# Attention block in fp16 pairs: row maxima of two heads at once on 64 rows each, and (1 + tanh) z on VectorE

## What is computed

```python
xn = jax.nn.silu(group_norm(x, gn_scale, gn_offset))        # 32 groups
qkv = jnp.einsum('bxyc,cd->bxyd', xn, w_qkv)
q, k, v = (to_heads(t) for t in jnp.split(qkv, 3, axis=-1))
sim = jnp.einsum('bhdi,bhdj->bhij', q * HEAD_CH ** (-0.5), k)
attn = jax.nn.softmax(sim, axis=-1)
out = jnp.einsum('bhij,bhdj->bhid', attn, v)
...
return jnp.einsum('bxyd,dc->bxyc', out, w_out) + b_out + x
```

## Time and profile before

| | us |
|---|---|
| median of 3 runs | 3589.93 |
| lowest and highest | 3588.99 and 3590.62 |
| the profiled execution | 3591.17 |
| its span | 3589.4 |
| PE busy | 3527.4 |
| VectorE busy | 2936.4 |
| ScalarE busy | 2738.4 |
| GpSimd busy | 2415.1 |

### The profile page before, as it was taken

One profiled execution on the slowest core, in us unless ns is written; L12 is line 12 of the kernel. 1 busy time (PEld: TensorE's weight loads), 2 busy tenths in 40 slices (PEclk: granted clock), 3 DMA queues, 4 the chain that ended last, 5 costly groups with the idle time before them and its releaser, 6 DMA issues.

```text
span 3589.4 us, 91303 instructions
## 1 busy us (share of the span) xinstructions
PE 3527.4 (98%) x31822; PEld 2074.5 (58%) x31822; DVE 2936.4 (82%) x3763; ACT 2738.4 (76%) x3076; POOL 2415.1 (67%) x2238
## 2 busy tenths in 40 slices
PE   6999999999999999999999999999999999999998
PEld 3555555565555556556565555555556555555555
DVE  7788878888788887888878888788888888878778
ACT  3787877878778787777877778787787877878776
POOL 1594866849578494775948659486684957849555
PEclk8999999999999999999999999999999999999999
DMA  3313323233232322223233232331323223232232
GB/s 97 71 36 97 68 42 94 54 83 65 50 86 53 83 65 64 72 59 93 48 73 80 45 97 42 97 68 42 95 53 83 65 52 85 53 83 65 43 92 47
DMA packets 178014, 245.82 MB, mean 68 GB/s; under 512 B 53536, under 2 KB 86304, under 8 KB 177568
## 3 DMA queue, kind: packets, MB, share of 16 engines
q1 hardware_dynamic: 177568, 239.94, 28.1%
HBM read 88.35 MB, written 33.82 MB: 34 GB/s over the span
## 4 chain that ended last, share of the span: by engine, by line
PE 89%; DVE 3%; POOL 3%; issue 3%; ACT 2%; DMA 0%; POOLq 0%; DVEq 0%; SPq 0%; ACTq 0%
PE SD L1160 33%; PE PV L1302 18%; PE TP L1175 11%; PE ST L1272 11%; PE ST L1273 11%; PE ST L1236 2%; PE ST L1243 1%; DVE mx L916 1%; POOL z L607 1%; ACT Ph L744 1%; DVE Pl L956 1%; POOL Pl L627 1%; POOL X L603 0%; POOL X L610 0%; PE SD L1225 0%
## 5 line engine op out<-in xcount | busy, mean ns | idle before, releaser
L627 POOL TENSOR_TENSOR Pl<-P,Ph 128x512 f16<-128x512 f32 x1024 | 1301.4, 1271 | 1091.7 <-ACT Ph L744 1091.0
L741 ACT ACTIVATE P<-ST,cns 128x1024 f32<-128x1024 f32 x1024 | 1141.9, 1115 | 774.5 <-PE ST L1273 700.2
L916 DVE TENSOR_REDUCE mx<-TP 128x1 f32<-128x1024 f32 x1024 | 1245.7, 1217 | 197.6 <-PE TP L1175 192.8
L744 ACT ACTIVATE Ph<-ST,cns 128x1024 f16<-128x1024 f32 x1024 | 1134.6, 1108 | 0.7 <-issue 0.7
L956 DVE TENSOR_TENSOR Pl<-P,Ph 128x512 f16<-128x512 f32 x1024 | 1029.6, 1005 | 39.3 <-ACT Ph L744 34.2
L1302 PE MATMUL PV<-V,Ph 128*128 128x129 f16 (+2 forms) x10240 | 862.0, 210 | 8.8 <-POOL Pl L627 4.0
L1302 PEld LDWEIGHTS PV<-V,Ph 128*128 128x128 f16 x10240 | 770.2, 97 | 134.5 <-issue 7.3
L1302 PE MATMUL PV<-V,Pl 128*128 128x65 f16 x8192 | 834.2, 192 | 0.0
L1302 PEld LDWEIGHTS PV<-V,Pl 128*128 128x128 f16 x8192 | 721.9, 98 | 109.4
L1272 PE MATMUL ST<-QK 128*128 128x512 f16 x2048 | 776.0, 379 | 3.0 <-DMA QK<-shift_rows 2.1
L1273 PE MATMUL ST<-QK 128*128 128x512 f16 x2048 | 776.3, 379 | 0.0
(11 more groups left out here) (133 smaller groups left out, 2878.4 us busy)
## 6 DMA issues: line engine op xcount, KB each, us to landing
QK<-QK SPq DMA_DIRECT2D x384, 256.0 KB, 4.9
x_in<-in_x SPq DMA_DIRECT2D x61, 512.0 KB, 3.6
res<-in_x SPq DMA_DIRECT2D x120, 256.0 KB, 4.6
out<-res SPq DMA_DIRECT2D x120, 256.0 KB, 3.3
V<-V SPq DMA_DIRECT2D x16, 1040.0 KB, 7.2
QK<-shift_rows SPq DMA_DIRECT2D x256, 64.0 KB, 3.4
shift_rows<-ms SPq DMA_DIRECT2D x256, 1.0 KB, 3.2
V<-in_L_conv_w_qkv SPq DMA_DIRECT2D x4, 768.0 KB, 10.1
```

Of the source, the lines that this page charges most:

```text
L627: nc.gpsimd.tensor_tensor(Pl[:, v % 4, HALF:], P32[:, v % 2, HALF:], Ph[:, v % 4, HALF:], ALU.subtract).then_inc(lo_pool, 1)
L741: nc.scalar.activation(P32[:, v % 2, :], ST[:, slot, :], ACT.Exp, scale=cns[:, 0:1])
L744: nc.scalar.activation(Ph[:, v % 4, :], ST[:, slot, :], ACT.Exp, scale=cns[:, 0:1]).then_inc(exp_done, 1)
L916: nc.vector.reduce_max(mx[:, hh, qb:qb + 1], TP[:], AX.X).then_inc(top_drained, 1)
```

## The change

**Maxima.** One batch is a block of 128 queries of both heads of a pair. In every even unit TensorE does four matmuls straight from the high parts in `QK`: for each half of the keys, head 0 on rows 0 to 63 into `TP` and head 1 on rows 64 to 127 into a slot of `ST`. Odd units have none. VectorE reduces the slot of `ST` in the even unit (`top_second`, counted by a new semaphore `top_read`) and `TP` in the odd one. The slot's use is an entry "top" of the ring. The maxima lead by 14 units; one shift serves both heads, with one DMA out and two back. The high parts of q and k have two buffers by the pair's parity.

**SiLU.** VectorE makes (1 + tanh) z (`gated`); GpSimd makes the high part by a multiplication by one, and the low part.

**Order.** Turns stand in odd units (one, at step 0 unit 3, after part 1). Out and v jobs stand in units 4 to 11. The start computes seven batches and one more q or k half.

```diff
-Q_HI, Q_LO, K_HI, K_LO = range(4)
+Q_HI, Q_LO, K_HI, K_LO = (0, 1), 2, (3, 4), 5
-TOP_LEAD = 8
+TOP_LEAD = 14
+def batch_of(step, u):
+    return divmod((16 * step + u + TOP_LEAD) // 2, TB)
 def unit_max(step, u, last=False):
-    head, qb = divmod(16 * step + u + TOP_LEAD, TB)
-    return [] if last and head == HEADS else [("max", head // 2 % 4, head % 2, qb)]
+    pair, qb = batch_of(step, u)
+    return [] if u % 2 or (last and pair == 4) else [("max", pair % 4, qb)]
-JOBS = [["qk"] * 3 + ["out"] * 4 + ["qk"], ["qk"] * 3 + ["out"] * 4 + ["qk"],
-        ["qk"] * 3 + ["v"] * 4 + ["qk"], ["qk"] * 3 + ["v"] * 4 + ["qk"]]
+JOBS = [["qk"] * 2 + [kind] * 4 + ["qk"] * 2 for kind in ("out", "out", "v", "v")]
-TURNS = {(0, 1): ("xt", 0), (0, 3): ("xt", 1), (0, 4): ("ot", 3), (0, 5): ("xt", 2), (0, 8): ("xt", 3),
-         (2, 0): ("ot", 0), (2, 8): ("ot", 1), (3, 4): ("ot", 2)}
+TURNS = {(0, 1): ("xt", 0), (0, 3): ("ot", 3), (0, 5): ("xt", 1), (0, 7): ("xt", 2), (0, 9): ("xt", 3),
+         (2, 1): ("ot", 0), (2, 9): ("ot", 1), (3, 5): ("ot", 2)}
 def maxima_first(u):
-    return u != 8
+    return u != 2
     for v in range(UNITS):
-        ring += [("score", v)] + unit_turn(v // 16, v % 16, first, last)
+        s, u = divmod(v, 16)
+        ring += [("score", v)] + [("top", v)] * len(unit_max(s, u, last)) + unit_turn(s, u, first, last)
+GATE_AT = [(1, 9), (1, 11), (1, 13), (2, 1), (2, 5), (2, 7), (2, 9), (2, 13)]
...
@@ SP: the shift's way
-                sp.dma_start(rows[half].rearrange("(p j) -> p j", j=4), ms[:, hh, 4 * half:4 * half + 4]
+                sp.dma_start(rows[half].rearrange("h (p j) -> p h j", j=4), ms[:, :, 4 * half:4 * half + 4]
                              ).then_inc(shift_row[half], 16)
+                for hh in range(2):
+                    sp.dma_start(QK2[rows_of(1 - hh), head_slot(pair, hh), 0, bass.ts(half, HALF)],
+                                 rows[half, hh:hh + 1].to_broadcast([HD, HALF])).then_inc(shift_placed[half], 16)
@@ GpSimd
+            def high_xn(image, par, i):
+                c, half = i % CC, i // CC
+                pool.wait_ge(xn_f32, PIECES * image + i + 1)
+                nc.gpsimd.tensor_tensor(xn[:, par, c, half, 0], z[:, i % 2], ones[:].to_broadcast([P, HALF]), ALU.mult
+                                        ).then_inc(xn_hi, 1)
@@ ScalarE: after exponentials and turn of unit u
+                    for _, qb in unit_shift(s, u, last):
+                        shift(qb // 4, cnt.top)
@@ VectorE
+            def top_second(use, cnt, slot):
+                qb = use[2]
+                dve.wait_ge(top_filled, cnt.top + 1)
+                nc.vector.reduce_max(mx[:, 1, qb:qb + 1], ST[:, slot], AX.X).then_inc(top_read, 1)
...
                         low_probs(b, v - 1)
+                    if (s, u) in GATE_AT and not last:
+                        gated(b + 1, GATE_AT.index((s, u)))
+                    cnt.next_slot()
                     for use in unit_max(s, u, last):
+                        top_second(use, cnt, cnt.next_slot())
+                    for use in unit_max(s, u - 1, last) if u > 0 else []:
                         top_use(use, b + 1, cnt)
@@ TensorE
                     for kh in range(2):
-                        ins = nc.tensor.matmul(TP[:, bass.ts(kh, HALF)],
-                                               QK1[:, slot, 0, qb // 4 * HALF + qb % 4:(qb // 4 + 1) * HALF:4],
-                                               QK1[:, slot, 1, bass.ts(kh, HALF)], start=True, stop=True)
+                        for hh, bank in enumerate((TP[:], ST[:, slot])):
+                            r = rows_of(hh)
+                            ins = nc.tensor.matmul(bank[:, bass.ts(kh, HALF)], QK[r, q_hi, block],
+                                                   QK[r, k_hi, bass.ts(kh, HALF)], start=True, stop=True)
...
                 if kind == "score":
                     pe.wait_ge(exp_done, UNITS * b + n + 1)
+                elif kind == "top":
+                    pe.wait_ge(top_read, BATCHES * b + TB + n // 2)
                 elif kind == "xt":
...
                 if v % 4 == 0:
-                    pe.wait_ge(shift_placed[q], 16 * HEADS * b + 16 * head + 16)
+                    pe.wait_ge(shift_placed[q], 128 * b + 32 * (head // 2) + 32)
+            def maxima(b, s, u, cnt, first, last):
+                for use in unit_max(s, u, last):
+                    wait_ring(("top", 16 * s + u), b, first, last)
+                    if use[2] == 0:
+                        pe.wait_ge(side_hi, cnt.hi)
+                    top_use(use, b, cnt, cnt.next_slot())
```

More of the change, by code:

```diff
@@ L93, in unit_job @@
     if kind == "qk":
-        ahead, n = divmod(j + 1, 8)
-        use = ("qk", (step + 1 + ahead) % 4, "qk"[n % 2], n // 2)
+        ahead, n = divmod(j + 2, 8)
+        use = ("qk", (step + 1 + ahead) % 4, *QK_ORDER[n])
         return [] if last and next_image(use, step) else [use]
     if kind == "out":
-        return [] if first else [("out", j - 3 + 4 * step)]
-    return [] if last else [("v", j - 3 + 4 * (step - 2))]
+        return [] if first else [("out", j - 2 + 4 * step)]
+    return [] if last else [("v", j - 2 + 4 * (step - 2))]
 def next_image(use, step):
@@ L220, in later @@
                      {kind: at + n["side"] for kind, at in self.mark.items()})
-TOPS_TO_MEAN = sum(use[0] in TOPS for use in PROLOGUE) + sum(len(unit_max(0, u)) for u in range(16)) + 3
+TOPS_TO_MEAN = sum(use[0] in TOPS for use in PROLOGUE) + sum(len(unit_max(0, u)) for u in range(16)) + 2
 assert len(ring_of()) % 2 == 0 and B % 2 == 0
@@ L489, in step @@
                         load_x(b + 2, 0)
-                    for n in unit_shift(s, u, last):
-                        place_shift(b, n)
+                    for pair, qb in unit_shift(s, u, last):
+                        place_shift(b, pair, qb // 4)
                     if u % 2 == 1:
@@ L653, in step @@
                         coefficients(b + 1)
-                    for i, op in [] if last else silu_ops(s, u):
-                        silu(b + 1, 1 - par, i, op)
+                    if not last:
+                        high, low = halves_at(s, u)
+                        for i in high:
+                            high_xn(b + 1, 1 - par, i)
+                        for i in low:
+                            low_xn(b + 1, 1 - par, i)
                     if (s, u) in BIAS_AT and not last:
@@ L776, in _ @@
                 turned(("xt", i), 0, 0, cnt)
+            for use in PROLOGUE:
+                if use[0] == "max":
+                    cnt.next_slot()
             def w_high(section):
@@ L801, in _ @@
                 side(use, 0, cnt, prologue_bank(cnt))
[L802 to L804 removed]
+                if use == ("v", 5):
+                    shift(0, sum(use[0] in TOPS for use in PROLOGUE[:PROLOGUE.index(("max", 0, 3)) + 1]))
             cnt.top = sum(use[0] in TOPS for use in PROLOGUE)
@@ L1250, in wait_ring @@
                 if at < 2:
-                    wait(pe, exp_done, UNITS * b - 1 + at)
+                    if at == 1 and not first:
+                        pe.wait_ge(exp_done, UNITS * b)
+                    else:
+                        pe.wait_ge(top_read, BATCHES * b + TB - 2 + at if first else BATCHES * b + TB - 1)
                     return
@@ L1320, in step @@
                         if maxima_first(u):
-                            for use in unit_max(s, u, last):
-                                top_use(use, image_of_tops(b, s, u), cnt)
+                            maxima(b, s, u, cnt, first, last)
                         if not (first and v < 2):
@@ L1332, in step @@
                     else:
-                        for use in unit_max(s, u, last):
-                            top_use(use, image_of_tops(b, s, u), cnt)
+                        for use in unit_job(s, u, first, last):
+                            side(use, image_of(use, b, s), par_of(use, s, par), cnt, part=1)
                         if turn_late(s, u):
                             turns(b, s, u, cnt, first, last)
-                        for use in unit_job(s, u, first, last):
-                            side(use, image_of(use, b, s), par_of(use, s, par), cnt, part=1)
                         for use in unit_part(s, u, last):
@@ L1374, in _ @@
                 if use[0] in TOPS:
-                    top_use(use, 0, cnt)
+                    wait(pe, side_drained, cnt.side - 1)
+                    wait(pe, top_read, use[2] - 1)
+                    top_use(use, 0, cnt, cnt.next_slot())
                 else:
```

132 lines of the change are left out of this document (55 added, 77 removed).

## The result

The changed kernel takes 3700.9 us (median; 3696.7 to 3706.8) against 3589.65: 1.031 times as long, 95% interval 1.030 to 1.033. The profiled execution's span is 3696.9 us against 3589.4.

What follows compares the result with a forecast made beforehand. The prediction took TensorE's own queue, busy 98% of the span, as the bound. It summed 3589.4 − 220 + 51 + 128 + 38 + 19 + 3 = 3608.4 us, forecast as 3609, range 3530 to 3725.

Steps and rivals of the forecast that it cites:

- pairs at once: TensorE's maxima on 64 rows: the two matmuls of each pair overlap, taking 220 us off the queue.
- to 64 rows and back: TensorE leaving its 128-row stream and returning, 512 batches at 0.10 us: 51 us (0 to 169).
- outputs' turns: In odd units; the next even unit's top waits for VectorE's low half: 8.1 us an image, 128 us, low bound 64.
- shift: Maxima's way through SBUF and DRAM and back: TensorE waits 1.2 us, 32 times, 38 us (0 to 90).
- ScalarE and VectorE late: Forecast as ScalarE's lateness: crowded units delay the next exponentials in five places, 1.2 us an image, 19 us (0 to 48).
- start: Kernel start: one projection and seven double batches in place of eight single ones, 3 us.
- the detour for the means: Group means on TensorE: two 4-column matmuls with two 32-bit weight loads, 0.20 us of queue, nearest guide to the switching price.
- the sign of being wrong: The prediction falls if a batch's switch to 64 rows and back costs outside 0 to 0.2 us.
- each way empties the array: Rival: switching to 64 rows and back costs 0.33 us a batch, 169 us, total 3700 us; chance 0.17.
- VectorE's room: VectorE's added (1 + tanh) z, 8 instructions of 0.685 us an image, fits under TensorE's queue: no cost unless VectorE is late.
- no wait over 0.3 us: Sign in the waits: TensorE shows none on exponentials longer than 0.3 us.

Runs made afterwards that it cites:

- e1: The changed kernel with each batch in the loop as two matmuls on all 128 rows instead of four on 64 rows; output not the reference's: 3629.6 us.
- e2: The changed kernel with the second pair of each batch behind P times V, so each batch goes to 64 rows and back twice: 3798.3 us.
- e3_top_behind: The changed kernel with the maxima behind P times V and projection part 0 in even units after a turn of the outputs: 3587.1 us.
- e5_shift_early: On top of e3_top_behind, the second half's shift taken one batch earlier, from blocks 3 to 6 instead of 4 to 7: 3545.0 us.
- e4_no_gate: The changed kernel with VectorE's (1 + tanh) z made on 4 of 512 columns in the loop; output not the reference's: 3709.1 us.

## Why the prediction was wrong

The forecast was 3609 us, within 3530 to 3725; slower was right and the time inside the range, but the slowdown was 19 us by forecast and 111 by measurement. The sum with the sizes that the runs show, on the span:

| term | forecast | measured | from |
|---|---|---|---|
| span before | 3589.4 | 3589.4 | page |
| pairs at once | −220 | −220 | starts of a pair, 0.01 us apart |
| to 64 rows and back | 51 | 111 | 0.22 us × 505; e1, e2 |
| outputs' turns | 128 | 163 | four units of an image longer by 2.8, 2.1, 3.0 and 2.5 us in the mean of images 1 to 14, times 63 / 4 |
| shift | 38 | 25 | waits |
| ScalarE and VectorE late | 19 | 25 | units (1, 0), (0, 2), (1, 2), (3, 2), (1, 8): 1.6 us an image |
| start | 3 | 4 | first score at 93.1, before at 88.7 |
| span after | 3608 | 3697 | page: 3696.9 |

The rows are read in different ways, so that they meet the span to 1 us is in part luck: the units behind the 63 turns themselves, with the shorter ones of the last image, add up to 157.

**The step that failed is the price of going to 64 rows and back.** I bounded it rightly (0 to 0.33) and then took 0.10, half of the detour for the means, on the argument that 16-bit loads are shorter. The measured 0.22 lies above the whole detour of 0.20, and outside the 0 to 0.2 us that I had named as the sign of being wrong. Going in costs 0.095 whether a matmul of 512 columns stands ahead (0.31 against 0.215) or, in `e2_two_ways`, P times V's last; coming back the same. The first weight load behind each change starts only with its matmul, where in a stream of whole rows it starts with the matmul before:

```profile
1708.46 0.11 PEld L1181 LDWEIGHTS TP<-QK 64*128 64x128 f16 x1 [0.42 <-issue]
1709.01 0.10 PEld L1311 LDWEIGHTS PV<-V,Ph 128*128 128x128 f16 x1 [0.41 <-issue]
```

In the trace of before, where a weight load stands so behind a wait, the next matmul follows after 0.24 us in place of 0.215; this 0.025 is the third part of the price. What holds the load and its matmul back for the 0.095, no run shows. It is less than the 0.164 us that a matmul's recorded length lies under the next, so an emptying in part would fit; but in the one batch of the changed kernel that enters 64 rows wholly at the lower clock (below), the first pair follows the last score after 0.564 us where a score follows after 0.427, and this 0.137 is not twice 0.095. The rival "each way empties the array" missed the price by as much on the other side (it charged 169 us for the way, which costs 111), and its total, 3700, is right by luck: the rest came from the terms below.
The Trainium skill (TensorEngine Tiling (Array Packing), Key Properties) says that a change of the tiling mode drains TensorE. The traces agree that a change costs, with 0.095 us each way; whether that is a drain they do not show.
The Trainium skill (TensorE: Matmul & The Clock Gate, Part 3) says that matmuls on different row groups run at once, some 4 ns apart. The trace agrees: the starts of a batch's first pair are 3 ns apart in the median, those of the second 1 ns, at most 34.

**The outputs' turns** were the right mechanism in the right place. A turn at (2, 9) of one image, timeline of VectorE and then TensorE:

```profile
1824.50 0.75 DVE L855 SCALAR_TENSOR_TENSOR V<-SD,sc,V 128x512 f16<-128x512 f32 x1
1825.17 1.22 DVE L883 TENSOR_TENSOR OT<-ST,OT 128x1024 f16<-128x1024 f32 x1
...
1823.97 0.38 PE L1282 MATMUL ST<-QK 128*128 128x512 f16 x1
1826.51 0.40 PE L1181 MATMUL TP<-QK 64*128 64x512 f16 x1 [2.16 <-DVE OT L883]
```

The low half of V goes first, then the turn's, and the top starts when that has ended: 2.54 us after the last score matmul where 0.31 is the least, 2.2 us lost against 2.3 in the working. The recorded waits are 114.4 us, and 119 when counted from the last matmul's start less its usual distance; the forecast was 128. (The list of weight loads has 12.1 us more for the same cause, but these are six of the same waits.) What I left out is what a wait does to the clock (below). A unit behind a turn is longer when it holds a stretch at the lower clock (unit 10 of step 2 takes 7.35 us with one and 5.75 without), by 35 us in the 23 units that do: 119 and 35 are nearly the 157.

**The shift** waited 34 times for 25 us; I had 32 times and 38 us. That later turns and slower batches moved TensorE's arrival would explain it, but is not shown. `e3_top_behind` and `e5_shift_early` show the full price: once the turns cover nothing, 42 us.

**VectorE's room** was judged rightly for the gate (`e4_no_gate`: nothing), by a size that was somewhat low: 0.82 us in the mean where the start's row said 0.685, though the middle one took 0.68 and the longest 1.65. But in one place VectorE was late without it: unit (1, 0), where aggregation and slow low parts (1.78 us, with GpSimd busy) push the reduction of TP 0.6 us past TensorE. I had said that the exponentials would cost no wait over 0.3 us; 16 waits come to 11.5 us, the longest 1.3.

**What the experiments leave.** With most of the turns' and the shift's waits taken away, the changed kernel is 1.4% faster than the one before. A period alone shows 0.20 us in 6.58 (3%); the difference is in waits that are left, on VectorE and ScalarE among others, and they are not added up here. That 1.4% contains shifts by another row's maximum, as said at `e5_shift_early`, and not by the row's own.

## What to carry to other kernels

Matmuls on half the rows run two at once, but each excursion from whole rows took back 0.22 of the 0.43 us that a batch of four such matmuls saves here: so count them, and let an excursion be long (a longer one was not tried here). In an in-order queue a new user of a shared buffer puts everything behind it under the slowest reader in the ring; before it is added, follow that reader's own queue, and stand the new work behind something that doesn't need the buffer. And in a kernel without a gap a wait can cost more than its length: here the granted clock fell behind 23 of the 62.

## What was not expected

The granted clock fell from 0.995 to 0.984 in the mean. Between the first scores and the last 4 us the trace before has no stretch at the lower level; the changed one has 25. Of these, 23 begin at a top that waited 1.5 to 2.2 us for a turn, from 0.1 us before the end of the wait to 1.5 us behind it. One begins behind a wait of 2.5 us for the shift's DMA in the first image, and one behind three waits of 1.3, 0.9 and 0.8 us within 6 us. One of the 23, the table by stretches (the clock is the column after POOL): at 1.00 while TensorE waits, at 0.50 (1.2 of 2.4 GHz) behind it, then back at 1.00.

```profile
2050.50:2054.50 4.00, 1.84 (x19) 0.70 (x17) 3.34 (x7) 3.92 (x6) 2.53 (x3) 1.00 0.04 1
2054.60:2058.00 3.40, 3.40 (x23) 1.75 (x20) 2.87 (x3) 0.00 (x0) 1.18 (x2) 0.50 0.33 43
2058.00:2062.00 4.00, 4.00 (x35) 2.08 (x35) 0.23 (x1) 2.83 (x4) 0.78 (x1) 1.00 0.00 0
```

In it six matmuls of a projection are recorded with 2.74 us; elsewhere they have 1.46:

```profile
2055.37 2.74 PE L1166 MATMUL SD<-wq,X 128*128 128x512 f16 x6
```

A mean of 0.984 against 0.995 is 0.011 × 3697 = 41 us of TensorE's full speed lost. Not every such wait is followed by a lower clock: 62 recorded waits for the turns, 23 stretches. With the waits removed (`e3_top_behind`), one stretch is left between the first scores and the last 4 us, in the first image.
